# A second input buffer in the query projection of a ternary transformer layer, paid for by normalizing in place

## The reference

```python
def bitlinear(x, W):
    sw = jnp.mean(jnp.abs(W)) + 1e-05
    Wq = jnp.clip(jnp.round(W / sw), -1.0, 1.0) * sw
    sx = 127.0 / jnp.clip(jnp.max(jnp.abs(x), axis=-1, keepdims=True), 1e-05, None)
    xq = jnp.clip(jnp.round(x * sx), -128.0, 127.0) / sx
    return jnp.einsum('bsd,od->bso', xq, Wq)

# x: (4, 4096, 2048) float32, 16 heads of 128, 4 key/value heads
xn = _layernorm(x, axis=-1)
q, k, v = bitlinear(xn, Wq), bitlinear(xn, Wk), bitlinear(xn, Wv)   # q, k rotated (rope)
...
attn = bitlinear(softmax(causal(q k^T / sqrt(128))) v, Wo)
ffn  = ((silu(xn @ gate_w.T * gate_s) * (xn @ up_w.T * up_s)) @ down_w.T) * down_s
out  = x + attn + ffn
```

## Time and profile before

| what | before |
|---|---|
| median of three runs | 5391.62 us |
| the profiled execution | 5419.9 us |
| its span on the slowest core (core 2) | 5418.4 us |
| spans of the 8 cores | 5359.2 to 5418.4 us |
| TensorE busy | 3840.3 us (71%) |
| VectorE busy | 1705.5 us (31%) |
| ScalarE busy | 1638.0 us (30%) |
| mean granted clock of TensorE, core 2 | 0.868 |
| `phase_b2`'s loop, first load issued to last store issued | 3071.4 to 3739.0 us |

### The profile page before, as it was taken

How to read it: one execution, slowest core, us unless ns; L and a number is a source line. 1 busy time by engine, 2 the same in 40 slices (tenths; PEclk the granted TensorE clock), 3 DMA queues, 4 the chain that set the end, 5 groups by cost and what they waited for, 6 DMA issues and landing times.

```text
span 5418.4 us, 55748 instructions; the slowest of 8 cores (5359.2 to 5418.4 us)
## 1 busy us (share of the span) xinstructions
PE 3840.3 (71%) x18728; PEld 1771.1 (33%) x18728; DVE 1705.5 (31%) x2837; ACT 1638.0 (30%) x1375; POOL 303.5 (6%) x276
## 2 busy tenths in 40 slices
PE   1799998979999899144445044545788889993188
PEld 1344443434444344132333033333222222222133
DVE  4111110111100000455555455655422211117533
ACT  4111110001111000533332622121455656663521
POOL 0111110101111010000000000000000000000000
PEclk9889998989999999566677577778999999995589
DMA  4799998999988697411110511111000000000366
GB/s 130 72 98 110 115 111 91 119 115 108 115 78 78 62 101 86 128 53 53 53 53 7 146 40 47 36 44 50 14 9 9 8 7 6 6 5 1 99 195 204
DMA packets 1047889, 387.68 MB, mean 72 GB/s; under 512 B 881856, under 2 KB 1025600, under 8 KB 1035328
## 3 DMA queue, kind: packets, MB, share of 16 engines
q0 software_dynamic: 548608, 161.50, 29.2%
q1 hardware_dynamic: 499008, 222.62, 18.1%
HBM read 480.53 MB, written 41.94 MB: 96 GB/s over the span
## 4 chain that ended last, share of the span: by engine, by line
PE 53%; DVE 18%; DMA 13%; ACT 9%; issue 5%; DVEq 1%; SPq 0%; ACTq 0%; POOLq 0%; POOL 0%
PE f_pg_h L340 10%; PE f_pu_h L346 10%; PE f_pd_h L386 9%; PE e_po L1007 4%; DMA pp_wb<-wq_t 3%; PE c_pse L800 3%; PE c_ppv L804 3%; ACT c_pp L858 2%; PE c_psc L849 2%; PE c_psc L847 2%; PE c_pse L802 2%; PE c_ppv L806 2%; PE b_pkv L618 2%; DVE b_sm L137 2%; DVE b_mx L166 2%
## 5 line engine op out<-in xcount | busy, mean ns | idle before, releaser
L858 ACT ACTIVATE c_pp<-c_psc 128x1024 bf16<-128x1024 f32 x640 | 655.4, 1024 | 581.4 <-PE c_psc L849 581.4
L340 PE MATMUL f_pg_h<-xnT,f_gw_h 128*128 128x512 bf16 x2816 | 643.6, 388 | 49.1 <-DMA f_uw_h<-uw_t 44.3
L386 PE MATMUL f_pd_h<-hdnT,f_dw_h 128*128 128x512 bf16 x2816 | 617.6, 381 | 46.6 <-DMA f_dw_h<-dw_t 44.4
L346 PE MATMUL f_pu_h<-xnT,f_uw_h 128*128 128x512 bf16 x2816 | 639.5, 387 | 0.0
L867 DVE TENSOR_TENSOR c_pp<-c_pp,cmask 128x512 bf16<-128x512 bf16 x512 | 217.7, 425 | 797.4 <-ACT c_pp L858 768.1
L715 PE MATMUL b_pq<-b_xqT,qtern 128*128 128x256 bf16 x2048 | 272.0, 293 | 266.2 <-DVE b_qrot L724 257.5
L340 PEld LDWEIGHTS f_pg_h<-xnT,f_gw_h 128*128 128x128 bf16 x2816 | 280.3, 100 | 398.0 <-issue 112.6
L386 PEld LDWEIGHTS f_pd_h<-hdnT,f_dw_h 128*128 128x128 bf16 x2816 | 276.1, 98 | 377.9 <-issue 55.4
L346 PEld LDWEIGHTS f_pu_h<-xnT,f_uw_h 128*128 128x128 bf16 x2816 | 279.5, 99 | 345.6 <-issue 56.9
L596 PE MATMUL b_pkv<-b_xqT,ktern 128*128 128x256 bf16 x1024 | 180.4, 359 | 287.7 <-DVE b_krot L605 270.9
L361 DVE TENSOR_TENSOR hdnT<-f_sg_h,f_su_h 128x1024 bf16<-128x1024 bf16 x88 | 60.9, 692 | 937.8 <-ACT f_su_h L357 937.8
(11 more groups left out here) (160 smaller groups left out, 3588.2 us busy)
## 6 DMA issues: line engine op xcount, KB each, us to landing
f_gw_h<-gw_t POOLq DMA_DIRECT2D x88, 512.0 KB, 8.9
f_uw_h<-uw_t POOLq DMA_DIRECT2D x88, 512.0 KB, 12.6
f_dw_h<-dw_t POOLq DMA_DIRECT2D x32, 1408.0 KB, 19.2
b_xch<-x_kv SPq DMA_DIRECT2D x16, 2048.0 KB, 7.7
f_xch<-x_q SPq DMA_DIRECT2D x4, 4096.0 KB, 16.8
pp_wb<-wq_t SPq DMA_DIRECT2D x64, 256.0 KB, 12.0
ffn_scr<-f_ffs_h SPq DMA_DIRECT2D x32, 512.0 KB, 4.9
pp_wb<-wo_t SPq DMA_DIRECT2D x64, 256.0 KB, 12.0
```

Source lines behind the costliest of these rows:

```text
L340: e.matmul(pg[:, bi, tc * 512:(tc + 1) * 512], gwb[wb][:, dt, :], xnT[:, dt, half * HT + tc * 512: half * HT + (tc + 1) * 512], start=(dt ...
L346: e.matmul(pu[:, bi, tc * 512:(tc + 1) * 512], uwb[wb][:, dt, :], xnT[:, dt, half * HT + tc * 512: half * HT + (tc + 1) * 512], start=(dt ...
L386: e.matmul(pd[:, pb, tc * 512:(tc + 1) * 512], dwb[wb][:, it, :], hdnT[:, it, tc * 512:(tc + 1) * 512], start=(it == 0), stop=(it == NIT - 1))
L858: E("scalar", lambda e, k0=k0, sbk=sbk: e.activation(pp[:, (k0 % 8):(k0 % 8) + 2, :].rearrange("p a b -> p (a b)"), psc[sbk][:], AF.Exp, s ...
```

## The change

Five edits, all in the diff below. In `phase_b2`, `xch` gets two buffers, chosen by the chunk's parity, and a load waits for the chunk before the last. The normalized rows are written in place, into `xch`, and the tile `xn_t` goes; `xi` and `xq` go from two buffers to one. `emit_quant_a` is split: `emit_quant_stat` has its three VectorE steps, `emit_quant_round` its two ScalarE steps. The order within a chunk is written out: on VectorE, `emit_quant_b` of tile 0 now stands ahead of the pending work of the chunk before, and the transposes of tile 0 stand behind that work; tile 1 follows as before. For all layer norms of the kernel, `ln_stats` puts the eight statistics into one tile, as column ranges of it.

```diff
     def ln_stats(stack, tag, junk, nt=4):
-        return dict(
-            sm=sb(f"{tag}_sm", [128, nt], F32, stack), ssq=sb(f"{tag}_ssq", [128, nt], F32, stack),
...
+        blk = sb(f"{tag}_stats", [128, 8 * nt], F32, stack)
+        names = ("sm", "ssq", "m", "msq", "var", "lnv", "rstd", "nb")
+        d = {nm: blk[:, i * nt:(i + 1) * nt] for i, nm in enumerate(names)}
...
+    def emit_quant_stat(xn_ap, mxv, sxv, tcol, xn_ready_w):
+        E("vector", lambda e: e.tensor_reduce(mxv[:, tcol], xn_ap, AX.X, ALU.max,
+                                              apply_absolute_value=True),
+          waits=[xn_ready_w, (ve, ve.n)], inc=(ve, 1))
...
+    def emit_quant_round(xn_ap, sxv, tcol, stat_ve, qst):
+        E("scalar", lambda e: e.activation(xn_ap, xn_ap, AF.Identity,
+                                           scale=sxv[:, tcol], bias=bC1),
+          waits=[(ve, stat_ve), (ac, ac.n)], inc=(ac, 1))
+        E("scalar", lambda e: e.activation(xi_t_of(qst, tcol), xn_ap, AF.Identity, bias=bmC1),
+          waits=[(ac, ac.n), (ve, qst["xi_ve"][_tc(tcol) % qst["nxi"]])], inc=(ac, 1))
+        return ac.n
...
-                xch = sb("b2_xch", [128, 1, 2, D], F32, b2)
-                xn_t = sb("b2_xn", [128, D], F32, b2)
-                xi_t = sb("b2_xi", [128, 2, D], I32, b2)
-                xq_t = sb("b2_xq", [128, 2, D], BF16, b2)
+                xch = sb("b2_xch", [128, 2, 2, D], F32, b2)
+                xi_t = sb("b2_xi", [128, 1, D], I32, b2)
+                xq_t = sb("b2_xq", [128, D], BF16, b2)
...
-                    E("sync", lambda e, c=c: e.dma_start(
-                        out=xch[:, 0, :, :], in_=x_q[c * 256:(c + 1) * 256, :]
+                    E("sync", lambda e, c=c, cb=cb: e.dma_start(
+                        out=xch[:, cb, :, :], in_=x_q[c * 256:(c + 1) * 256, :]
                         .rearrange("(t p) f -> p t f", p=128)),
-                      waits=[(ve, xch_done[0][0]), (ac, xch_done[0][1])], inc=(s_x[cb], 16))
+                      waits=[(ve, xch_done[cb][0]), (ac, xch_done[cb][1])], inc=(s_x[cb], 16))
...
+                    nac0 = b2_norm(0)
+                    sve0 = emit_quant_stat(xch[:, cb, 0, :], mxv, sxv, slice(0, 1), (ac, nac0))
+                    ra0 = emit_quant_round(xch[:, cb, 0, :], sxv, slice(0, 1), sve0, qst)
+                    nac1 = b2_norm(1)
+                    sve1 = emit_quant_stat(xch[:, cb, 1, :], mxv, sxv, slice(1, 2), (ac, nac1))
+                    emit_quant_b(xq_t[:], mxv, slice(0, 1), ra0, qst)
+                    rdy0 = (ve, ve.n)
+                    ra1 = emit_quant_round(xch[:, cb, 1, :], sxv, slice(1, 2), sve1, qst)
                     if pend[0] is not None:
                         pend[0]()
                         pend[0] = None
-                    for t in range(2):
...
+                    b2_tr(0, rdy0)
+                    emit_quant_b(xq_t[:], mxv, slice(1, 2), ra1, qst)
+                    b2_tr(1, (ve, ve.n))
+                    xch_done[cb] = (ve.n, ac.n)
```

More of the change, by code:

```diff
@@ L124, in ln_stats @@
     def ln_stats(stack, tag, junk, nt=4):
-        return dict(
-            sm=sb(f"{tag}_sm", [128, nt], F32, stack), ssq=sb(f"{tag}_ssq", [128, nt], F32, stack),
[L127 to L131, removed]
+        blk = sb(f"{tag}_stats", [128, 8 * nt], F32, stack)
+        names = ("sm", "ssq", "m", "msq", "var", "lnv", "rstd", "nb")
+        d = {nm: blk[:, i * nt:(i + 1) * nt] for i, nm in enumerate(names)}
+        d["junk"] = junk
+        d["nt"] = nt
+        return d
     def emit_ln(xch, stats, wait_load, per_tile_fn=None):
@@ L179, in emit_quant_a @@
         return ac.n
+    def emit_quant_stat(xn_ap, mxv, sxv, tcol, xn_ready_w):
+        E("vector", lambda e: e.tensor_reduce(mxv[:, tcol], xn_ap, AX.X, ALU.max,
+                                              apply_absolute_value=True),
+          waits=[xn_ready_w, (ve, ve.n)], inc=(ve, 1))
+        E("vector", lambda e: e.tensor_scalar(mxv[:, tcol], mxv[:, tcol], 1e-5, 1.0 / 127.0,
+                                              ALU.max, ALU.mult),
+          waits=[(ve, ve.n)], inc=(ve, 1))
+        E("vector", lambda e: e.reciprocal(sxv[:, tcol], mxv[:, tcol]),
+          waits=[(ve, ve.n)], inc=(ve, 1))
+        return ve.n
+    def emit_quant_round(xn_ap, sxv, tcol, stat_ve, qst):
[5 more added lines that the diff above has]
+        return ac.n
     def _tc(tcol):
@@ L189, in emit_quant_b @@
                                               ALU.mult),
-          waits=[(ac, round_ac), (pe, qst["tr_pe"][_tc(tcol) % 2])], inc=(ve, 1))
+          waits=[(ac, round_ac), (pe, qst["tr_pe"][_tc(tcol) % qst.get("ntr", 2)])], inc=(ve, 1))
         qst["xi_ve"][_tc(tcol) % qst["nxi"]] = ve.n
@@ L663, in phase_b2 @@
                 rope_done = [ve.n, ve.n]
-                qst = dict(tr_pe=[pe.n, pe.n], xi_ve=[ve.n, ve.n], xi=xi_t, nxi=2)
+                qst = dict(tr_pe=[pe.n], xi_ve=[ve.n], xi=xi_t, nxi=1, ntr=1)
                 xn_ve = [ve.n, ve.n]
@@ L683, in phase_b2, with b2_norm, b2_tr @@
                     E("vector", None, waits=[(pe, xqT_pe[0])])
-                    stat_done = emit_ln(xch[:, 0, :, :], stats, ldw)
-                    round_acs = []
-                    for t in range(2):
-                        tp = t % 2
-                        E("scalar", lambda e, t=t, cb=cb, tp=tp: e.activation(
-                            xn_t[:], xch[:, 0, t, :], AF.Identity,
-                            bias=stats["nb"][:, t:t + 1], scale=stats["rstd"][:, t:t + 1]),
[L691 to L695, removed]
+                    stat_done = emit_ln(xch[:, cb, :, :], stats, ldw)
+                    def b2_norm(t, cb=cb):
+                        E("scalar", lambda e, t=t, cb=cb: e.activation(
+                            xch[:, cb, t, :], xch[:, cb, t, :], AF.Identity,
+                            bias=stats["nb"][:, t:t + 1], scale=stats["rstd"][:, t:t + 1]),
+                          waits=[stat_done, (ac, ac.n)], inc=(ac, 1))
+                        return ac.n
+                    def b2_tr(t, rdy):
+                        emit_tr16(xq_t[:],
+                                  lambda g, t=t: xqT[:, 0, g * 8:(g + 1) * 8,
+                                                     t * 128:(t + 1) * 128],
+                                  ptr, rdy, t, ptr_ve, extra_w=[(pe, xqT_pe[0])])
+                        qst["tr_pe"][0] = pe.n
+                    nac0 = b2_norm(0)
[6 more added lines that the diff above has]
+                    ra1 = emit_quant_round(xch[:, cb, 1, :], sxv, slice(1, 2), sve1, qst)
                     if pend[0] is not None:
```

## The result

The changed kernel takes 0.9918 of the time of the kernel before, with a 95% interval of 0.9903 to 0.9933. Of 5391.6 us that is 44 us less (36 to 52); the forecast was 46.6. By this ratio the changed kernel takes 5347 us, against the 5345 foretold; its profiled execution took 5345.65.

What follows compares the result with a forecast made beforehand. The prediction took `phase_b2` as a chain on VectorE, its loads held by one buffer. Savings of 8.9 + 44.1 + 2.6 less 9.1 gave 46.6 unrounded: 5391.6 - 46.6 = 5345 us, range 5323 to 5365.

Steps and rivals of the forecast that it cites:

- What bounds the stage: Query projection `phase_b2`: no engine is full; a chain through VectorE, which waits 68.9 us for loads of `b_xch`.
- The load of chunk 1: Second load of `phase_b2`: with two buffers it goes out right behind load 0, hidden under chunk 0; saves 8.9 us.
- Load 0: First load of `phase_b2`, 9.71 us from issue to row sum: not delayed by load 1 going out behind it; nothing charged.
- The loads of chunks 2 to 7: In `phase_b2`, issued 8.1 us earlier, behind 16 stores; stretch from last rotation to row sum 9.4 us, was 16.8; saves 44.1.
- the 0.75 for the two tables: Delay in us of each load of chunks 2 to 7 by two rope table loads issued beside it; bounds 0 and 1.5.
- The moved quantization: Tile 0's quantization ahead of the rotations in `phase_b2`: adds 1.3 us in chunks 1 to 7, no wait; 9.1 lost.
- The last stretch: After chunk 7 of `phase_b2`, from last rotation to last copy: 8.5 us become 5.9; saves 2.6.
- The edits costed at nothing: In-place normalization, one `xq` buffer, packed statistics in 28 layer norms: 0 us, the statistics bounded by 8 either way.
- The signs: Profile after, in `phase_b2`: chunk about 77 us, load within 0.2 of last store, wait 3 to 4 in each of six chunks.
- Full hiding: Rival: all loads of `phase_b2` hidden, each stretch 6.0 us instead of 16.8; gain 67, total 5324; chance 0.07.
- The late landing: Rival: loads of `phase_b2` land later than reckoned, each microsecond costing six; at 4 more the gain is 23; chance 0.11.
- The slower clock in the attention stage: Rival: attention stage after `phase_b2` drops from clock 0.99 to 0.94, costing 52 us; chance 0.04.

Runs made afterwards that it cites:

- the last run above: Changed kernel with each load issued ahead of the stores and three of 16 pending heads' rotations moved into VectorE's waits for ScalarE's normalization: loop 544.9 us, ratio to before 0.9832.

## Why the prediction was right

*What bounds the stage.* Right: VectorE's list with its waits, and the load behind it. Filling two waits, in the last run above, shortened the loop by 54.6, within 2 us of that run's working.

*The load of chunk 1.* Right: its wait is gone, 8.9. Load 0, charged nothing, takes 10.8 us to its row sum on average over the cores where it took 10.3; the cores range from 9.6 to 12.6, and from 9.4 to 11.2 before, so the 0.5 is not told from nothing.

*The loads of chunks 2 to 7.* The mechanism was right, one size was off. The load is issued 0.55 us after the last rotation (0.45 foretold), and VectorE is free after 5.45 (5.9). But from issue to row sum it takes 10.07 + 0.16 = 10.2 on average where the sum had 8.21 + 0.75. So the stretch is 10.8 against 9.4, and the saving 6 x (16.8 - 10.8) = 36 instead of 44.1. The term that was mis-sized is the 0.75 for the two tables: it was taken as half of what four tables seemed to cost load 0, and the runs show that the price does not go by the number of tables: on single cores 2.2 for two (10.07 less 7.91) and 2.4 for four (10.34 less 7.91), over eight cores 1.9 and 2.4. Both halves of that step erred: four tables cost 2.4 and not 1.5, and two cost most of what four do and not half. The 9.71 that the 1.5 came from was one core's load 0; the eight average 10.3. Both figures for two tables lie outside the bounds of 0 and 1.5. Some 0.5 of the 1.9 are the long loads, which nothing in the working foresaw. By the Trainium skill's rule of turns between queues (DMA: Bandwidth & Descriptors, "Queues, rings and completion order") a second queue delays the load, as it does here; the estimate of 0.6 from bytes and that page's fabric rate is too low against the 1.9 to 2.2 measured.

*The moved quantization.* Right. On core 0 of the changed kernel:

```profile
3098.11 0.16 DVE L187 RECIPROCAL b_sx<-b_mx 128x1 f32<-128x1 f32 x1
3098.28 1.29 DVE L206 TENSOR_SCALAR b_xq<-b_xi,b_mx 128x2048 bf16<-128x2048 int32 x1
...
3099.67 0.42 DVE L742 TENSOR_TENSOR b_q<-b_pq,ccqs 128x256 f32<-128x256 f32 x1
```

1.40 us from the end of the reciprocal to the first rotation, where the earlier trace rows had 0.11: 1.29 in seven chunks, 9.0. VectorE waited once for integers in the whole loop, for 0.2 us, as before.

*The last stretch.* 8.5 - 5.45 = 3.0 against 2.6. *The edits costed at nothing:* the packed statistics measured nothing; the in-place form takes 2.09 us like the other.

*Sum.* 8.9 + 36 + 3.0 - 9.0 = 38.9, and the loop lost 39.9. This compares one core of either kernel; over all eight the stretch fell from 16.95 to 10.61, 38.0 for six, and the sum is 40.9, or 40.4 with the 0.5 of load 0. The interval of the whole, 36 to 52, holds this and the forecast. That the forecast of 46.6 lies so near to the 44 of the whole is in part luck: the loop, where all terms of the sum lie, lost 6.7 less than foretold.

*The signs.* One chunk takes 77.7 us (3143.51 to 3221.17), 77 foretold, and the load follows the last store by 0.16. The wait in the six chunks is 5.3, over the 3 to 4 foretold but under the 6 that would have meant the rival.

*The rivals.* Full hiding did not happen, and for the reason given: with the load ahead of the stores it does, and brings 29.8 more. The late landing is what happened in a small dose, 1.3 us in six chunks on core 0. The slower clock in the attention stage did not come: 0.99, and the stage as long as before.

## What to carry to other kernels

A second buffer frees a load only as far as its place in the issuing queue allows: look at what stands ahead of it there and what that waits for, and put the load ahead of stores that wait for late work. An order that is right while one wait sets the stretch can be wrong once another does: price a moved instruction against the wait that is left, not against the one that was there. When a stage is one engine's list with waits in it, look for pending work that can stand in the waits; here that brought more than the buffer.

## What the runs showed of the hardware

Two loads of 128 KB on GpSimd's queue delay a 2 MB load on SyncE's by 1.9 us on average over eight cores (10.06 against 8.14 from issue to row sum), four by 2.4, one by 1.5, and the same two from ScalarE's queue, the first issued 0.5 us earlier, by 0.8. A price by bytes would have been even.

Where a packet of 16 KB of the `instruction` queue started 8.67 to 9.14 us after the load's issue, the load took 11.1 to 11.5 us to its row sum in place of 9.1 to 10.0 (15 loads of 48); one other, with the packet at 8.73, took 9.6.

GpSimd's issue of a table takes 0.54 us, but 1.43 where it fell together with VectorE's quantization: L695 ran from 3221.71 to 3223.14, L206 from 3221.74 to 3223.01. The Trainium skill (SBUF — State Buffer, "SBUF: two separate sides") says that a VectorE instruction in a two-port mode keeps GpSimd from writing descriptors until it ends; the 0.13 us between the two ends here agrees, but no run shows in which mode L206 ran. No wait for a table shows in the loop: the tables are needed a chunk later.
